# Cached keys turned in 32x32 blocks by VectorE instead of by TensorE, in a fused four-layer kernel

## What is computed

```python
q = einsum('bsd,ed->bse', x, Wq).reshape(8, 128, 32, 128)      # 32 query heads
k, v = ...                                                     # 8 key/value heads of 128
q, k = _rope(_rmsnorm(q, q_norm_w), pos), _rope(_rmsnorm(k, k_norm_w), pos)
kc = k_cache[block_table].reshape(bsz, 512, 8, 128)            # 16 pages of 32 cached keys
vc = v_cache[block_table].reshape(bsz, 512, 8, 128)
k_all, v_all = concatenate([kc, k], 1), concatenate([vc, v], 1)     # 640 keys
scores = where(valid, einsum('bqhd,bkhd->bhqk', q, k_all) * SCALE, -1e30)
o = einsum('bhqk,bkhd->bqhd', softmax(scores), v_all)
x = x + einsum('bse,de->bsd', o.reshape(bsz, 128, 4096), Wo)
```

## Time and profile before

| | us |
|---|---|
| median of 3 runs | 1533.02 (1532.79 to 1535.52) |
| the profiled execution | 1530.62 |
| its span, first to last instruction | 1528.9 |
| PE busy | 1434.5 (94%) |
| DVE busy | 1163.2 (76%) |
| ACT busy | 939.4 (61%) |
| POOL busy | 493.7 (32%) |
| granted TensorE clock, mean | 0.992 of full speed |

### The profile page before, as it was taken

How to read it: one execution, slowest core, us unless ns; L and a number is a source line. 1 busy time by engine, 2 the same in 40 slices (tenths; PEclk the granted TensorE clock), 3 DMA queues, 4 the chain that set the end, 5 groups by cost and what they waited for, 6 DMA issues and landing times.

```text
span 1528.9 us, 29324 instructions
## 1 busy us (share of the span) xinstructions
PE 1434.5 (94%) x8014; PEld 1230.2 (80%) x8014; DVE 1163.2 (76%) x2800; ACT 939.4 (61%) x1860; POOL 493.7 (32%) x678
## 2 busy tenths in 40 slices
PE   3998999788999899999999999999999999999988
PEld 2776887667788788888878887888788888888767
DVE  4675767566688788778878886888788778888756
ACT  2333232356677677767767776777677667777643
POOL 4243000155543333333433333343333333433200
PEclk9999999999999999999999999999999999999999
DMA  8678642345321112111111111021112111111214
GB/s 179 207 240 283 197 150 89 98 126 159 111 63 49 50 29 63 60 40 49 50 47 45 57 56 51 29 63 49 51 29 63 60 40 49 50 42 36 97 60 161
DMA packets 104275, 131.03 MB, mean 86 GB/s; under 512 B 11861, under 2 KB 79590, under 8 KB 98838
## 3 DMA queue, kind: packets, MB, share of 16 engines
q1 hardware_dynamic: 98678, 109.49, 23.6%
q0 software_dynamic: 5024, 17.93, 3.9%
q10 hardware_dynamic: 384, 1.41, 0.7%
HBM read 125.63 MB, written 36.72 MB: 106 GB/s over the span
## 4 chain that ended last, share of the span: by engine, by line
PE 75%; issue 9%; DVE 7%; ACT 2%; POOL 2%; DMA 2%; POOLq 1%; SPq 1%; ACTq 0%; DVEq 0%
PE proj_ps L1170 16%; PE sc L1210 12%; PE o_ps L1247 12%; PE proj_ps L1268 11%; PE ring L1229 8%; PE proj_ps L1026 4%; PE o_ps L1026 4%; PE sc L1026 3%; PE ring L1283 2%; PE ring L1295 1%; PE ring L1026 1%; DMA wd_raw<-in_WdT 1%; POOLq L584 1%; DVE w_l L1426 1%; POOL v_pages L585 1%
## 5 line engine op out<-in xcount | busy, mean ns | idle before, releaser
L1699 DVE TENSOR_TENSOR pTl<-ring,pTh 128x512 fp32r<-128x512 f32 x320 | 215.1, 689 | 72.8 <-ACT pTh L851 69.3
L833 ACT ACTIVATE p_sb<-p_sb,bias,rstd 128x640 f32<-128x640 f32 x256 | 235.8, 921 | 46.7 <-DVE bias L1675 46.7
L637 POOL TENSOR_TENSOR rstd<-var,half_neg 128x4 f32<-128x4 f32 x64 | 80.6, 1259 | 532.1 <-DVE var L1736 483.5
L851 ACT ACTIVATE pTh<-ring 128x512 fp32r<-128x512 f32 x320 | 184.4, 599 | 55.2 <-PE ring L1229 54.4
L1665 DVE CUSTOM_DVE_ANT_0 p_sb<-sc,mask 128x640 f32<-128x640 f32 x256 | 209.1, 817 | 4.4 <-PE sc L1210 0.8
L1229 PE MATMUL ring<-ident,p_sb 128*128 128x128 f32 x1280 | 183.5, 274 | 5.7 <-DVE p_sb L1691 3.4
L1170 PE MATMUL proj_ps<-wh,xh 128*128 128x512 f32 (+1 forms) x512 | 179.7, 351 | 8.9 <-issue 8.2
L1229 PEld LDWEIGHTS ring<-ident,p_sb 128*128 128x128 f32 x1280 | 153.9, 141 | 33.5 <-DVE p_sb L1691 3.7
L1170 PE MATMUL proj_ps<-wl,xh 128*128 128x512 f32 (+1 forms) x512 | 172.6, 337 | 0.0
L1170 PE MATMUL proj_ps<-wh,xl 128*128 128x512 f32 (+1 forms) x512 | 172.2, 336 | 0.0
L1210 PE MATMUL sc<-kTh,qTh 128*128 128x320 f32 x512 | 163.5, 319 | 1.8 <-DVE kTl L1800 1.8
(11 more groups left out here) (247 smaller groups left out, 3632.7 us busy)
## 6 DMA issues: line engine op xcount, KB each, us to landing
k_pages<-in_k_cache SPq DMA_DIRECT2D x128, 128.0 KB, 3.4
v_pages<-in_v_cache POOLq DMA_DIRECT2D x128, 128.0 KB, 3.5
k_raw<-k_pages SPq DMA_DIRECT2D x64, 256.0 KB, 3.1
v_raw<-v_pages SPq DMA_DIRECT2D x64, 256.0 KB, 3.0
stage<-in_Wqkv SPq DMA_DIRECT2D x32, 384.0 KB, 3.5
w_raw<-in_WguT SPq DMA_DIRECT2D x20, 512.0 KB, 5.7
stage<-in_WoT SPq DMA_DIRECT2D x32, 256.0 KB, 3.3
w_raw<-in_W3T SPq DMA_DIRECT2D x8, 1024.0 KB, 5.4
```

What stands on the lines that cost most here:

```text
L833: act_e.activation(p_sb[:, p_slot(u, h), :], p_sb[:, p_slot(u, h), :], ACT.Exp, bias=bias[:, h:h + 1], scale=rstd[:, u.k % 2, h:h + 1], ac ...
L851: act_e.activation(pTh[:, c, :], ring[c % 2][:, :], ACT.Copy).then_inc(S["pth"], 1)
L1699: v.tensor_tensor(pTl[:, c, :], ring[c % 2][:, :], pTh[:, c, :].bitcast(F32), ALU.subtract).then_inc(S["ptl"], 1)
```

## The change

The load of the cached keys becomes four DMAs, one for each 32 features. DMA j puts, for each of the 16 pages, the 32 keys of the page on partitions 32j to 32j+31 and their features 32j to 32j+31 beside each other (pieces of 32 numbers, 128 bytes). So each 32x32 block already stands where its turned form belongs, and only has to be turned in itself. DVE does that for all 64 blocks in one instruction, `k_raw` to the new tile `k_turned` in SBUF, between `cos_k` and `low_pt(2)`. PE's `transpose_keys` is gone with its PSUM bank. ACT reads `k_turned` for `kTh`, now ahead of `square_q`. The low half leaves DVE and is made by POOL between `k_pow` and `q_pow`. `transpose_new` on PE takes over the waits that `transpose_keys` had for its bank.

```diff
-        k_raw = l1_sb("k_raw", [P, LC, D])
+        k_raw = l1_sb("k_raw", [P, L])
...
+        k_turned = l1_sb("k_turned", [P, L])
...
-                sp.dma_start(k_raw[:, :, :], of_head(k_pages, u)).then_inc(k_load, 16)
+                pages = k_pages[u.seq, :, :, :].rearrange("(i r) h d -> r i (h d)", r=PSIZE)
+                for j in range(D // PSIZE):
+                    sp.dma_start(k_raw[j * PSIZE:(j + 1) * PSIZE, :].rearrange("r (i c) -> r i c", c=PSIZE),
+                                 pages[:, :, bass.ds(u.head * D + j * PSIZE, PSIZE)]).then_inc(k_load, 16)
...
+                pool.wait_ge(S["kch"], u.count(1, 1))
+                pool.tensor_tensor(kTl[:, u.k % 2, 0:L], k_turned[:, :], kTh[:, u.k % 2, 0:L].bitcast(F32), ALU.subtract
+                                   ).then_inc(S["kcl"], 1)
                 pool.wait_ge(S["q_var"], u.count(1, 1))
...
-                act_e.activation(kTh[:, u.k % 2, 0:L], ring[1][:, :], ACT.Copy).then_inc(S["kch"], 1)
+                act_e.activation(kTh[:, u.k % 2, 0:L], k_turned[:, :], ACT.Copy).then_inc(S["kch"], 1)
...
                 high_pt(u + -2, 4)
+                high_cached_k(u)
                 square_q(u)
                 new_wqkv(u + 1, 1)
-                high_cached_k(u)
                 new_wo(u + -2, 3)
...
-            def transpose_keys(u):
-                if not u.exists():
-                    return
-                pe.wait_ge(k_load, u.count(16, 16))
...
-                for c in range(LC):
-                    i = nc.tensor.transpose(ring[1][:, c * P:(c + 1) * P], k_raw[:, c, :], ident[:, :])
-                i.then_inc(S["kcT"], 1)
-
...
                 pe.wait_ge(S["krope"], u.count(1, 1))
-                pe.wait_ge(S["kcl"], u.count(1, 1))
+                if u.back(2):
+                    pe.wait_ge(S["ptl"], (u + -2).count(KC, 4))
...
                 attend(u + -2, 2)
-                transpose_keys(u)
                 attend(u + -2, 3)
...
-            def low_cached_k(u):
...
-                v.tensor_tensor(kTl[:, u.k % 2, 0:L], ring[1][:, :], kTh[:, u.k % 2, 0:L].bitcast(F32), ALU.subtract
-                                ).then_inc(S["kcl"], 1)
+            def turn_cached_k(u):
+
+                if not u.exists():
+                    return
+                dve.wait_ge(k_load, u.count(4 * 16, 4 * 16))
+                if u.back(1):
+                    dve.wait_ge(S["kcl"], u.count(1, 0))
+                v.transpose(k_turned[:, :], k_raw[:, :]).then_inc(S["kcT"], 1)
...
                 cos_k(u)
+                turn_cached_k(u)
                 low_pt(u + -2, 2)
...
-                low_cached_k(u)
```

More of the change, by code:

```diff
@@ L1270, in output @@
                 i.then_inc(S["y"], 1)
-            def transpose_keys(u):
-                if not u.exists():
-                    return
-                pe.wait_ge(k_load, u.count(16, 16))
-                if u.back(2):
-                    pe.wait_ge(S["ptl"], (u + -2).count(KC, 4))
-                elif u.k == 0:
-                    pe.wait_ge(S["x1l"], HALF)
-                else:
-                    pe.wait_ge(S["knl"], u.count(1, 0))
-                for c in range(LC):
-                    i = nc.tensor.transpose(ring[1][:, c * P:(c + 1) * P], k_raw[:, c, :], ident[:, :])
-                i.then_inc(S["kcT"], 1)
             def transpose_queries(u):
@@ L1301, in transpose_new @@
                 pe.wait_ge(S["krope"], u.count(1, 1))
-                pe.wait_ge(S["kcl"], u.count(1, 1))
+                if u.back(2):
+                    pe.wait_ge(S["ptl"], (u + -2).count(KC, 4))
+                elif u.k == 0:
+                    pe.wait_ge(S["x1l"], HALF)
+                else:
+                    pe.wait_ge(S["knl"], u.count(1, 0))
                 nc.tensor.transpose(ring[1][:, 0:P], k_cos[:, :], ident[:, :]).then_inc(S["knT"], 1)
@@ L1737, in mean_square_q @@
                                 ).then_inc(S["q_var"], 1)
-            def low_cached_k(u):
+            def turn_cached_k(u):
                 if not u.exists():
                     return
-                dve.wait_ge(S["kch"], u.count(1, 1))
-                v.tensor_tensor(kTl[:, u.k % 2, 0:L], ring[1][:, :], kTh[:, u.k % 2, 0:L].bitcast(F32), ALU.subtract
-                                ).then_inc(S["kcl"], 1)
+                dve.wait_ge(k_load, u.count(4 * 16, 4 * 16))
+                if u.back(1):
+                    dve.wait_ge(S["kcl"], u.count(1, 0))
+                v.transpose(k_turned[:, :], k_raw[:, :]).then_inc(S["kcT"], 1)
             def cos_k(u):
```

## The result

| | before | changed |
|---|---|---|
| median of 13 runs, taken side by side (us) | 1534.18 | 1539.15 |
| lowest to highest | 1530.95 to 1539.31 | 1537.11 to 1544.61 |
| span of the profiled execution | 1528.9 | 1537.4 |
| that execution's own time | 1530.62 | 1539.04 |

The ratio is 1.004, 95% interval 1.0027 to 1.0053: on 1533 us that is 6 us slower (4 to 8). 3.6 us were forecast. The changed kernel ran once more later (`e14_after`) and gave 1.0027.

The account below looks back on a forecast made before the run. TensorE bounds it, never waiting in a plain step, with the last chunk's chain PE, ACT, DVE, PE just in time. Plain steps +1.3 and new-weight steps +2.3 make +3.6 us: 1534.2, moved by 2.4 to 1536.6; range 1529 to 1563.

Parts of the forecast that it names:

- The turn: DVE's turn of the cached keys ahead of `low_pt(2)`: one pass, 0.61 us plus 0.04 for filling a block, 0.65.
- double pass: Rival: every element passes DVE twice in the turn, 1.16 us to the next instruction; +30 us, 1563; chance 0.16.
- fast turn: Rival: DVE's turn runs at the rate of `L1691`, 0.38 us to the next instruction; -3 us, 1530; chance 0.08.
- What stands in the way: Ahead of `attend(4)`, PE waits for the last chunk through ACT and DVE; of 0.45 us freed, 0.08 is left.
- +0.03 us in a plain step: `attend(4)` starts 0.03 us later in each of 44 plain steps, because the turn delays `low_pt(2)`: +1.3 us.
- the matmul 0.19 after that: On PE at `attend(4)`: the first matmul starts 0.19 us after its weight load, so not before 843.03.
- +0.33 us in a step with new weights: DVE has no idle time before `low_pt(4)`, so `attend(4)` comes 0.33 us later in seven steps: +2.3 us.
- The seven first steps and the six at the turns of the loop ... zero.: These steps wait later for POOL and ACT anyway, by up to 4.6 and 2.3 us, and take up the shift.
- What moves and costs nothing: Moved work is covered: POOL's added 1.31 us a step lies where `q_pow` waits 8.3 us a step for DVE.
- Hidden, with 3 us to spare: SP's load of keys in four DMAs takes 13.5 us at most, needed by the next turn 16.6 us later.
- The rival of small pieces: 128-byte pieces make the key load 25.9 us against 16.6; DVE waits 9.3 us in some 57 steps; 2060; chance 0.04.
- PE's full gain: Rival: PE gets back all 0.45 us a step of the removed transposes; -23 us, 1510; chance 0.06.

Follow-up runs that it names:

- e14_after: The changed kernel itself, nothing altered, run once more later beside other follow-up runs: 1539.78 us, ratio 1.0027 to the kernel before.
- e3_pe: Changed kernel with TensorE doing all of the second half of the scores, `scores(2)`, before the last attention chunk, `attend(4)`: 1544.57 us, ratio 1.005 to the kernel before.
- e10_half: Changed kernel with only the first half of `scores(2)`, three matmuls, moved ahead of `attend(4)` on TensorE: 1536.22 us, ratio 0.9999 to the kernel before.
- e1_gate: Changed kernel with one added wait (the gate): GpSimd's subtraction starts only when VectorE's `scale_k` has ended; 1531.48 us, ratio 0.9972 to the kernel before.
- e2_sp: Changed kernel with the last quarter of a step's Wo load issued a step later, behind the load of cached keys: 1539.62 us, ratio 1.0032 to the kernel before.
- e7_onedma: Changed kernel with keys loaded by one DMA of 512-byte pieces again, so the multiplied keys are wrong: 1545.5 us, ratio 1.0073 to the kernel before.

## Why the prediction was right and wrong

The range held, and so did the main trait of the picture of a plain step, the wait ahead of `attend(4)`. The right sign and the near number are luck: the two terms of the sum, with the sizes that the trace gives them, are 44 x -0.11 and 7 x +0.14 us, which makes the kernel 3.8 us faster and not 3.6 slower. It is slower through what the prediction put at zero: the first steps (+5.7), and the port and the late load in the k = 2 and k = 0 steps (+6.3 and +1.9 in all), against the steps with a turn of the loop (-4.9). One of its own signs of being wrong was met as well: DVE waits for a DMA, in seven steps.

- **The turn** was given 0.65 us to the next instruction, and the trace has 0.63 (846.68 to 847.31). The double pass and the fast turn are out.
- **What stands in the way** was right: PE waits ahead of `attend(4)` in place of the transposes, 71 waits and 35.0 us in all (some 50 of about 0.4 were forecast). `e3_pe` and `e10_half` confirm that this chain, and right behind it the one over `oTh` and `oTl`, decide.
- **+0.03 us in a plain step** was measured as -0.11. The step that failed is "the matmul 0.19 after that". A matmul that has waited is shown from its load's start, and the next one comes 0.34 later instead of 0.23 (850.08, 850.42), so the restart costs 0.11 and not 0.19: 0.08 of the 0.14 between forecast and trace. The rest came from `low_pt(2)`, which began 0.03 us earlier than forecast, took 0.65 us instead of 0.69, and pulled the chain forward by 0.07.
- **+0.33 us in a step with new weights** was measured as +0.14 (123.9 to 124.9 in seven): right sign, too large. DVE ended the last low half 0.22 us later there, not 0.33, and the restart was 0.08 cheaper.
- **"The seven first steps and the six at the turns of the loop ... zero."** Both are wrong: +5.7 and -4.9 us. The first is GpSimd's subtraction holding up `scale_k` (`e1_gate`). Of the second, 4.0 stand in the lists of waits: PE's seven waits for `oTh`, six of them at the turns, fell from 14.8 to 10.8 us. ACT, idle at its own turn of the loop, begins the `vh` behind it 12.49 us into unit 27's step, where it was 13.29, and `oTh` follows. What brings ACT there earlier was not tested.
- **"What moves and costs nothing"**: POOL's added 1.31 us was covered on POOL, as said, but the sentence looked only at who waits for POOL, not at what DVE can't do meanwhile. That is +5.6 us in the first steps and +1.9 in the k = 0 steps, recovered by the gate to 127.0 and 120.2.
- **"Hidden, with 3 us to spare"** took the load to be issued as soon as the turn before it was done, 16.6 us ahead. In seven steps SP stands elsewhere. The sentence on "slightly late loads" was attached to the seven steps whose load stands behind the stage loads and priced at a few us. It was the right spot and belonged in the sum: of the +6.3 us in the k = 2 steps, the earlier issue alone took back 4.5 (`e2_sp`), and the gate alone 2.6.
- **The rival of small pieces** is out: 4.9 us against 4.8 for the old form in the same unit. The Trainium skill's rule on transfers below 512 bytes (DMA: Bandwidth & Descriptors, Specifications) did not lengthen this load of 256 KB. In the DMA engines' busy share the small pieces do show, 0.16 of a plain step against 0.11 in `e7_onedma`.
- **PE's full gain**, given 0.06, was excluded as the program stood, and rightly; `e10_half` shows that one exchange of three matmuls makes it true in the plain steps.

## What to carry to other kernels

When an operation is moved to a resource that has idle time, look at three things besides its own length: what shares a port with it, what is queued in front of its load on the issuing engine when the data are needed earlier than before, and which chain takes up the freed time. An instruction that is blocked at a port is shown as a longer one, so compare the mean lengths of instructions that were *not* changed, not only the waits. Freed time on the critical engine comes back only if other work fills the new gap, and just as much as fits: half of `scores(2)` did, the whole of it pushed the next chain.

## What the runs showed of the hardware

- A VectorE instruction of 0.28 us (`sum_k`, `scale_k`) that begins during a GpSimd subtraction over two SBUF inputs lasts until that has ended and 0.08 to 0.15 us more: 1.40 and 1.22 us, in 57 units of the changed kernel. GpSimd's own stays at 1.25 to 1.30 where nothing of VectorE's came first. Where VectorE's began 0.01 to 0.05 us earlier, it kept its 0.28, and GpSimd's took 1.38 to 1.42 (11 units).
- VectorE turns 64 float32 blocks of 32x32 in one instruction of 704 ns, about what a subtraction of as many elements takes (685 ns from SBUF).
- SP takes 1.9 to 2.0 us to issue four DMAs of 64 KB in 128-byte pieces, 0.37 for one of 256 KB in 512-byte pieces, and both sets were there 4.8 to 4.9 us after the first issue in unit 26, with stage loads beside them. For the same bytes the small pieces keep the DMA engines busy longer, 0.16 of a plain step against 0.11.
- A turn of the hardware loop is not a fixed price. The six steps with a turn have equal instructions in one kernel and took 20.3 to 21.2 us in the changed one and 21.3 to 21.9 in the one before, against 17.2 to 17.3 for a plain step.
